# A four-stage kernel on one core: GpSimd's subtract behind VectorE's turn, the turn's transfers first, row statistics at a later beat

## The reference, cut to what matters

```python
def _L1_xattn_ref(q, k, v):          # q = layernorm(x), k = v = ctx; 256 rows x 512 each
    h = 8
    qh = q.reshape(b * h, d // h, m)   # 8 heads of 32 rows
    kh = k.reshape(b * h, d // h, -1)
    vh = v.reshape(b * h, c // h, -1)
    scale = 1.0 / jnp.sqrt(jnp.asarray(d // h, dtype=q.dtype))
    qk = jnp.einsum('bdm,bdn->bmn', qh, kh) * scale     # 512 x 512 for each head
    sm = jax.nn.softmax(qk, axis=-1)
    ret = jnp.einsum('bmn,bcn->bcm', sm, vh)
    return ret.reshape(b, c, m)

x = x + jnp.tanh(g_xattn[1]) * _L1_xattn_ref(_layernorm(x, axis=-1), ctx_2048, ctx_2048)
```

## Time and profile before

| | |
|---|---|
| Median of three runs | 1604.55 us |
| Profiled execution, its own time | 1603.89 us |
| Its span | 1602.2 us |
| Busy: TensorE matmuls | 1505.0 us, 94% |
| Busy: VectorE | 1211.6 us, 76% |
| Busy: GpSimd | 1021.9 us, 64% |
| Busy: ScalarE | 964.5 us, 60% |
| First to last matmul of the first pass (L1442) | 528.0 to 988.5 us |
| First to last matmul of the second pass (L1456) | 545.1 to 1008.4 us |

### The profile page before, as it was taken

How to read it: one execution, slowest core, us unless ns; L and a number is a source line. 1 busy time by engine, 2 the same in 40 slices (tenths; PEclk the granted TensorE clock), 3 DMA queues, 4 the chain that set the end, 5 groups by cost and what they waited for, 6 DMA issues and landing times.

```text
span 1602.2 us, 28275 instructions
## 1 busy us (share of the span) xinstructions
PE 1505.0 (94%) x8801; PEld 1071.2 (67%) x8801; DVE 1211.6 (76%) x1964; ACT 964.5 (60%) x1497; POOL 1021.9 (64%) x791
## 2 busy tenths in 40 slices
PE   4999999998887899999999999898999999999996
PEld 3677777776553644444444444488989999999995
DVE  7788888888827678888888886285777777777775
ACT  5433232233824378888888887646667777677773
POOL 4788888885406578888888887402555555555553
PEclk9999999999998799999999999999999999999998
DMA  7234444444763877778777871571443444444443
GB/s 260 98 131 142 144 144 144 143 134 105 214 157 134 191 186 194 194 196 208 195 199 193 207 199 56 202 285 41 79 74 73 80 80 80 79 76 75 77 78 54
DMA packets 114972, 224.27 MB, mean 140 GB/s; under 512 B 17088, under 2 KB 17088, under 8 KB 113984
## 3 DMA queue, kind: packets, MB, share of 16 engines
q1 hardware_dynamic: 98400, 185.10, 40.5%
q0 software_dynamic: 15904, 37.23, 12.9%
q10 hardware_dynamic: 576, 0.79, 0.2%
HBM read 146.71 MB, written 75.84 MB: 139 GB/s over the span
## 4 chain that ended last, share of the span: by engine, by line
PE 28%; DMA 22%; DVE 7%; issue 5%; ACT 2%; POOL 2%; SPq 0%; ACTq 0%; DVEq 0%; POOLq 0%
DMA out_rows<-XN,slots 20%; PE pB L1456 6%; PE pO L1466 6%; PE pA L1442 6%; DVE low L1793 4%; PE pB L1476 3%; PE pA L1602 2%; DMA XN<-normed_rows,slots 1%; PE pO L1614 1%; PE pB L1614 1%; POOL out_rows L1424 1%; ACT inv L1645 1%; PE pA L1519 1%; DVE split L1781 1%; PE pB L1535 1%
## 5 line engine op out<-in xcount | busy, mean ns | idle before, releaser
L1793 DVE TENSOR_REDUCE low<-pA 128x2 f32<-128x1024 f32 x256 | 303.4, 1218 | 65.4 <-PE pA L1442 63.0
L1424 POOL DMA_INDIRECT out_rows<-XN,slots x71 | 200.4, 2822 | 211.8 <-DMA out_rows<-XN,slots 167.8
L436 PE MATMUL y<-kv,toep 128*128 128x288 f32 x1280 | 326.1, 411 | 9.0 <-DVEq L63 5.8
L1684 ACT ACTIVATE pt<-pB 128x512 f32<-128x512 f32 x512 | 281.0, 599 | 69.3 <-PE pB L1456 65.7
L436 PEld LDWEIGHTS y<-kv,toep 128*128 128x128 f32 x1280 | 238.0, 190 | 96.9 <-DVEq L63 34.1
L1602 PEld LDWEIGHTS pA<-XN,fc 128*128 128x128 f32 x2272 | 265.6, 192 | 10.9 <-issue 5.6
L1602 PE MATMUL pA<-XN,fc 128*128 128x128 f32 x2272 | 266.4, 276 | 5.0 <-DVE XN L1958 4.0
L1456 PE MATMUL pB<-qs,ks 98*128 98x512 f32 x512 | 215.0, 433 | 0.9 <-ACT pt L1684 0.7
L1442 PE MATMUL pA<-ks,qs 96*128 96x512 f32 x512 | 190.1, 410 | 9.1 <-DVE low L1793 3.8
L1387 POOL TENSOR_TENSOR part_sum<-pt 128x1024 f32<-128x1024 f32 x64 | 152.8, 2388 | 68.6 <-ACT pt L1684 66.1
L406 ACT ACTIVATE ym<-y 128x384 f32<-128x384 f32 (+1 forms) x128 | 52.6, 411 | 228.9 <-PE y L436 228.9
(11 more groups left out here) (294 smaller groups left out, 2500.6 us busy)
## 6 DMA issues: line engine op xcount, KB each, us to landing
ks<-ctx_high SPq DMA_DIRECT2D x62, 256.0 KB, 4.7
qs<-q_high SPq DMA_DIRECT2D x62, 256.0 KB, 6.3
kc<-in_ctx_conv SPq DMA_DIRECT2D x32, 384.0 KB, 5.3
XN<-in_x SPq DMA_DIRECT2D x16, 512.0 KB, 10.2
toep<-kernel_and_skip SPq DMA_DIRECT2D x32, 256.0 KB, 3.4
ct<-in_ctx SPq DMA_DIRECT2D x16, 512.0 KB, 6.4
ctx_high<-kh SPq DMA_DIRECT2D x16, 512.0 KB, 4.4
ctx_low<-kl SPq DMA_DIRECT2D x16, 512.0 KB, 5.1
```

The source lines that it names most:

```text
L436: m = pe.matmul(y[half].rearrange("p (l n) c -> p l n c", l=CB)[:, l, :, 0:PAIRS], toep[u][:, (l - s) * P:(l - s + 1) * P], kv[u][:, half, ...
L1424: pool.indirect_dma_start(out=out["out"], out_offset=bass.IndirectOffsetOnAxis(ap=slots[:, j:j + 1], axis=0), in_=ys[j % 2], in_offset=Non ...
L1684: act.activation(pt[s][:, h, :], pB[n % 3], ACT.Exp, scale=SCALE1).then_inc(s_exp, 1)
L1793: dve.tensor_reduce(low[u % 2][:, 2 * n:2 * n + 2], pA[n % 2], op=ALU.max, axis=AX.X, negate=True).then_inc(s_red, 1)
```

## The change

Three edits, all in the attention loop. GpSimd's `query_low(j)`, called in the body of unit j - 4, waits also for s_sp to reach 3 (j - 3) + 3, which is the end of the transpose in `halves` for unit j - 3; a `sem_inc` on s_go goes with the second wait. SyncE's body issues `shift(j + 1)` ahead of `store_query(j + 4)`. VectorE's body takes `measure(j - 2)` behind beat 15 instead of beat 7.

```diff
@@ SyncE, body
                     load(j + 3, n)
+                if exists(j + 1):
+                    shift(j + 1, (u + 1) % TRIP)
                 if exists(j + 4):
                     store_query(j + 4)
-                if exists(j + 1):
-                    shift(j + 1, (u + 1) % TRIP)
                 if exists(j - 2):
                     store(j - 2, (u + 2) % TRIP)
@@ GpSimd
             def query_low(j):
                 pool.wait_ge(s_q, 2 * j - 6)
+                pool.wait_ge(s_sp, 3 * (j - 3) + 3)
+                pool.sem_inc(s_go, 1)
                 pool.tensor_tensor(nextl.bitcast(F32R), nextq, nexth, ALU.subtract).then_inc(s_ql, 1)
@@ VectorE, body
                     if beat == 3 and exists(j - 4):
                         refine(j - 4, u)
-                    if beat == 7 and exists(j - 2):
+                    if beat == 15 and exists(j - 2):
                         measure(j - 2, (u + 2) % TRIP)
                     if beat == 11 and exists(j - 1):
                         scale(j - 1)
```

## The result

The changed kernel takes 1588.66 us (median of four runs, 1588.03 to 1589.43) against 1605.04 us for the kernel before (median of four, 1604.52 to 1606.98). The ratio is 0.9899 with a 95% interval of 0.9870 to 0.9927: faster by 1.0%, 16.4 us by the medians. The profiled execution has a span of 1587.0 us, 15.2 us less than before.

The account below looks back on a forecast made before the run. VectorE's turns, held by GpSimd's subtract, were taken to keep the attention loop from TensorE's own pace. Gains of 13.7 + 1.7 = 15.4 us gave 1589.2, written as 1589.5 us for a few hitches; range 1587.5 to 1597.

Parts of the forecast that it names:

- edit 2: SyncE issues the maxima's transfers before the query stores: nothing in the loop, 1.7 us gained at its start.
- What bounds the loop: In the attention loop, held turns are all that separates the mean unit, 14.585 us, from TensorE's own 14.06 us.
- edit 1: GpSimd's subtract waits for VectorE's turn in each unit: 26 x 0.525 us, 13.7 us gained, low end 5.9.
- rival B: The change doesn't reach the path, something else fills the gap: time within 3 us of 1604.5; chance 0.05.
- the count by casts: In the attention loop, 30 casts take 0.453 us each beyond their free 0.17 us: 13.6 us.
- The wake-up: GpSimd's delay from the end of VectorE's turn to its subtract: 0.25 us, with ends of 0.18 and 0.42.
- The ring's room of 0.17 us: GpSimd's cycle of turn, subtract, sums, addition and next cast closes with 0.17 us between addition and cast.
- the cover: Slack on GpSimd before the later subtract would delay the first part sum: 0.1 us, or minus 0.07.
- Rival A: GpSimd becomes the bound, or its addition holds the cast: units 14.2 to 14.35 us, 1593 to 1597; chance 0.14.
- the wait should go altogether: At the loop's start, TensorE's 1.66 us wait for unit 1's maxima disappears: 1.7 us gained.
- Edit 3: Row statistics on VectorE move from beat 7 to beat 15: value 0, ends 0 and a loss of 2 us.
- C: Statistics at beat 15 are held by GpSimd's part sums: 1.1 us a unit lost, time near 1620; chance 0.04.

Follow-up runs that it names:

- dose: Changed kernel with a second GpSimd subtract, into a tile nobody reads, behind the wait for the turn: half width 1595.42 us, full width 1605.13 us.
- only_wait: Kernel before with only GpSimd's wait for the turn added: median 1591.62 us, ratio 0.9905.
- no_stats_move: Changed kernel with the row statistics back behind beat 7: 1589.03 us, ratio 0.9899.
- dose_full: Changed kernel with a second, full-width GpSimd subtract behind the wait and ahead of the real one: median 1605.13 us, ratio 0.9995.

## Why the prediction was right, point by point

**Range and time.** Forecast 1589.5, range 1587.5 to 1597, measured 1588.66. The sum was 15.4 us; the medians differ by 16.4 and the spans by 15.2. The 13.7 us of the loop are understood. That the whole comes as close is partly luck: outside the loop the spans differ by 2.2 us gained at its start, 1.6 lost ahead of it and 0.9 gained behind it, all within what these stretches scatter, and no run shows the 1.7 us of edit 2.

**What bounds the loop.** Right: casts free and units at 14.06 to 14.07 us in every kernel that has edit 1 and no dose. But one reading was wrong. Under rival B the pairs of units without a held cast were said to be all within 0.1 us of 14.06. In one of them, in the kernel before, it is the small subtract that is held, and the next cast comes 14.90 us later:

```profile
742.56 0.17 DVE L1781 CAST split<-low 128x16 fp32r<-128x16 f32 x1
742.77 1.13 DVE L1783 TENSOR_TENSOR split<-low,split 128x16 fp32r<-128x16 f32 x1
...
757.46 0.46 DVE L1781 CAST split<-low 128x16 fp32r<-128x16 f32 x1
```

It supports the mechanism, but the count by casts, 13.6 us, left it out and met the 13.7 us so closely partly by luck. With it the holds are 26 x 0.55 = 14.3 us for 13.7 lost, so nearly the whole of a hold, not all, went into the unit.

**Edit 1, 13.7 us.** Right in size: 26 x (14.585 - 14.063) = 13.6 us, and only_wait shows that it is this edit alone. The wake-up put at 0.25 us was 0.18 (turn's end at 709.59, subtract at 709.77). The first part sum stayed at t0 + 2.53.

**The ring's room of 0.17 us was mis-sized.** 0.17 us is where a first hold would begin. But a longer ring first uses up slack inside it. A cast that is held ends with the addition, so the addition's end and the next subtract lie 0.76 us apart and not 0.90. And the first part sum no longer waits for ScalarE: it starts 1.24 us behind the start of the subtract and not 1.63, so that the cover I had put at 0.1 us and the 0.18 us between instructions are gone too. That is 0.53 us beside the 0.17: the doses showed 0.7 us. Rival A was therefore further off than its 0.14: by this reading another 0.3 us in the ring would have cost nothing in the unit, with a ring of 13.66 us against 14.06. No run has just that.

**Edit 2, nothing in the loop, 1.7 us at its start.** In the loop right. At the start the step "the wait should go altogether" failed: 1.09 us of it was left.

```profile
562.63 0.19 PEld L1458 LDWEIGHTS pB<-qs,ks 98*128 98x128 f32 x1 [1.09 <-DMA qs<-turned]
```

This answers the earlier trace rows. The start got shorter by 2.2 us all the same, in this execution. I had taken TensorE's arrival as fixed. It isn't. With the new order the wait for unit 1's maxima was 1.09 to 2.77 us in five of the seven starts and absent in two (no_stats_move, dose_full), and these two took 29.14 and 29.50 us, longer than the 28.20 here. TensorE's wait for unit 2's queries was 3.4 to 3.9 us in four of the eleven executions, with a granted clock of 0.50 to 0.61 behind it, and 1.3 us or less in the others. What decides between these starts stays open.

**Edit 3, nothing.** Right on top of edit 1 (0.2 us in 26 units). Without edit 1 it is worth 5.3 us, which I hadn't priced; I had written that it adds slack behind the turn and given it no number. The fit at beat 15 was better than the 0.14 us forecast: 0.78 us of idle time is left behind the statistics. VectorE reaches them 0.33 us earlier in the unit (t0 + 7.98 instead of 8.31), and they keep it for 0.92 us, since 0.22 of the 1.24 us at beat 7 was a wait behind them.

**Rivals B and C.** B is out by edit 1 alone. C is out by the statistics' 683 ns, though GpSimd's sums run beside them in each unit. The four steps of refining, for which the prediction charged nothing, stayed free as well.

## What to carry to other kernels

When a tiny VectorE instruction has a mean several times its free time, lay its timeline beside GpSimd's: here 0.55 us of hold, once a unit, was the whole distance to TensorE's own pace, while VectorE was idle for a seventh of the time and GpSimd for a sixth. One wait on GpSimd, behind the short VectorE instructions, turned idle time of GpSimd into that gain. Before trusting such a ring, stretch it with a dose: the room that a timeline shows is the room to the first touch, not to the first loss.

## What the runs showed of the hardware that I had not expected

Each of the two short instructions can be the one that is held, whichever is next when GpSimd's instruction is running: the cast (1.17 us instead of 0.17) or the subtract of two SBUF tiles (1.15 us instead of 0.17). Refining the statistics, with 128x1 operands, was held in no unit of the two kernels: in the changed one the last step began at 721.56, inside the addition that began at 721.48, and took 0.21 us. And GpSimd's start behind VectorE's signal was quick, 0.18 or 0.19 us with a second wait in front of it in 24 of 27 units, and 0.27 us in the first three.
